# One program for weight folding and the first batch's chain, in an attention kernel on one core

## The reference

```python
xn = _layernorm(x)
kv_c = xn @ W_kvd + b_kvd
q_c = xn @ W_qd + b_qd
q = concatenate([q_c @ W_qu + b_qu, rope(q_c @ W_qr + b_qr)])
k = concatenate([kv_c @ W_ku + b_ku, rope(kv_c @ W_kr + b_kr)])
probs = softmax(where(causal, -1e9, q k^T * scale))
ctx = probs @ (kv_c @ W_vu + b_vu)
out = x + ctx @ W_o + b_o + xn @ bw^T + bias
```

## Time and profile before

| | |
|---|---|
| time, median of 3 runs | 1512.25 us (1511.94 to 1512.78) |
| time of the profiled execution | 1512.11 us |
| its span | 1510.3 us |
| TensorE busy | 1434.2 us, 95% |
| VectorE, ScalarE, GpSimd busy | 1159.1, 1210.5, 947.1 us |
| first instruction of `layer` on TensorE | 97.35 us |
| first instruction of the first step on TensorE | 148.04 us |

### The profile page before, as it was taken

How to read it: one execution, slowest core, us unless ns; L and a number is a source line. 1 busy time by engine, 2 the same in 40 slices (tenths; PEclk the granted TensorE clock), 3 DMA queues, 4 the chain that set the end, 5 groups by cost and what they waited for, 6 DMA issues and landing times.

```text
span 1510.3 us, 27896 instructions
## 1 busy us (share of the span) xinstructions
PE 1434.2 (95%) x9878; PEld 1300.2 (86%) x9878; DVE 1159.1 (77%) x2764; ACT 1210.5 (80%) x2565; POOL 947.1 (63%) x476
## 2 busy tenths in 40 slices
PE   1976999999999999999999999999999999999998
PEld 1855899999889999999889899999889999999987
DVE  2444688888677888888767788888767788888887
ACT  1532788889868888889878888899878888888886
POOL 3010777776767677777767577776866567777750
PEclk9996999999999999999999999999999999999998
DMA  8445232222132432222033432221123422111110
GB/s 209 160 162 124 60 88 60 60 60 60 26 88 71 109 88 60 61 60 60 18 81 84 109 88 60 61 59 46 30 74 95 109 60 60 47 48 49 52 29 29
DMA packets 46819, 111.62 MB, mean 74 GB/s; under 512 B 13600, under 2 KB 22816, under 8 KB 46688
## 3 DMA queue, kind: packets, MB, share of 16 engines
q1 hardware_dynamic: 36912, 103.31, 25.1%
q10 hardware_dynamic: 8720, 3.70, 1.1%
q0 software_dynamic: 1056, 2.89, 0.7%
HBM read 50.10 MB, written 13.63 MB: 42 GB/s over the span
## 4 chain that ended last, share of the span: by engine, by line
PE 81%; ACT 4%; DVE 4%; SPq 1%; POOL 1%; DMA 1%; issue 1%; DVEq 0%; POOLq 0%; ACTq 0%
PE turn L1355 16%; PE ring L1300 11%; PE u_ps L1373 8%; PE ring L1332 8%; PE u_ps L1374 8%; PE ring L1330 8%; PE ring L1331 8%; PE o_ps L1393 4%; PE o_ps L1394 4%; PE ring L1313 2%; PE ring L1262 2%; PE ring L1268 1%; ACT probs L886 1%; DVE probs L1067 1%; DVE probs_lo L1077 1%
## 5 line engine op out<-in xcount | busy, mean ns | idle before, releaser
L1067 DVE TENSOR_SCALAR_CACHE_REDUCE probs<-ring,c_t 128x1024 f32<-128x1024 f32 (+7 forms) x512 | 413.8, 809 | 106.5 <-PE ring L1332 104.1
L1077 DVE TENSOR_TENSOR probs_lo<-turn,probs_hi 128x512 fp32r<-128x512 f32 (+1 forms) x640 | 401.0, 630 | 68.9 <-ACT probs_hi L895 64.2
L895 ACT ACTIVATE probs_hi<-turn 128x512 fp32r<-128x512 f32 (+1 forms) x640 | 351.0, 550 | 113.7 <-PE turn L1355 108.9
L886 ACT ACTIVATE probs<-probs,row_min 128x1024 f32<-128x1024 f32 (+7 forms) x512 | 394.3, 771 | 12.1 <-DVE probs L1067 9.5
L1355 PE MATMUL turn<-ident,probs 128*128 128x128 f32 x2304 | 385.4, 275 | 6.0 <-ACT probs L886 3.7
L1373 PE MATMUL u_ps<-probs_hi,kv_nat 128*128 128x256 f32 x1152 | 314.8, 302 | 0.3 <-DVE probs_lo L1077 0.3
L1355 PEld LDWEIGHTS turn<-ident,probs 128*128 128x128 f32 x2304 | 286.5, 140 | 31.9 <-ACT probs L886 8.9
L1374 PE MATMUL u_ps<-probs_lo,kv_nat 128*128 128x256 f32 x1152 | 290.1, 281 | 0.0
L1330 PE MATMUL ring<-k_hi,q_hi 128*128 128x512 f32 (+2 forms) x768 | 279.8, 364 | 0.0
L1332 PE MATMUL ring<-k_hi,q_lo 128*128 128x512 f32 (+2 forms) x768 | 264.3, 344 | 0.0
L1331 PE MATMUL ring<-k_lo,q_hi 128*128 128x512 f32 (+2 forms) x768 | 262.8, 342 | 0.0
(11 more groups left out here) (174 smaller groups left out, 2623.1 us busy)
## 6 DMA issues: line engine op xcount, KB each, us to landing
wp<-wp_scratch SPq DMA_DIRECT2D x32, 640.0 KB, 4.2
wv<-wv_scratch SPq DMA_DIRECT2D x32, 512.0 KB, 3.4
swapped<-k_rope SPq DMA_DIRECT2D x128, 128.0 KB, 2.3
swapped<-q_y SPq DMA_DIRECT2D x64, 128.0 KB, 2.3
swapped<-q_x SPq DMA_DIRECT2D x64, 128.0 KB, 2.3
wp_scratch<-wp_parts SPq DMA_DIRECT2D x8, 640.0 KB, 3.4
wv_scratch<-wv_parts SPq DMA_DIRECT2D x8, 512.0 KB, 4.2
k_hi<-qb_kv_hi SPq DMA_DIRECT2D x16, 256.0 KB, 3.8
```

The source lines that it names most:

```text
L886: act.activation(p, p, ACT.Exp, scale=-1.0, bias=row_min[:, r:r + 1], accum_out=row_sum[:, g % 4, w, h:h + 1]).then_inc(exp_ready, 1)
L895: act.activation(probs_hi[:, r % 4, 0:width], turn[r % 2][:, 0:width], ACT.Identity).then_inc(turned_hi, 1)
L1067: dve.tensor_scalar(probs_of(g, w, h), ring[slot_of(entry)][:, KEY_COLUMN[qt]:KEY_COLUMN[qt] + keys], c_t[b % 2][:, qt, ds(pair * 2 + h, 1 ...
L1077: dve.tensor_tensor(probs_lo[:, r % 4, 0:width], turn[r % 2][:, 0:width], probs_hi[:, r % 4, 0:width].bitcast(F32), ALU.subtract).then_inc ...
```

## The change

`prepare` and `layer` become one block. The heads are folded one by one, and the chain of the first batch stands between them on every engine.

- TensorE turns heads 0 and 1, then for each i folds head i and turns head i + 2. Behind head 1 come the transposes, behind 2 the down matmuls, behind 5 the projection of the first pair, behind 8 the bias sums, behind 12 and 13 the linear map, and natural at the end. Turned heads lie in the PSUM tensors `turn`, folded ones in `u_ps` and `o_ps`, one head in each.
- ScalarE makes the high parts straight from PSUM (`folded_high`), VectorE the low parts (`folded_low`), both into the parts of the pair. The first pair's parts are `wp` and `wv[0]` themselves; they are stored, but not loaded in the prologue.
- GpSimd scales the rotary weights once and makes their high and low parts (`rope_columns`), and issues the stores (`store_parts`). Before the parts of a pair are written again, the engine that writes waits for the store (`wait_stored`).
- The biases are loaded as rows and turned by one TensorE transpose (`bias_columns` copies them out). x, these rows, the heads, `w_down` and half of W_o are loaded by SP; the other half of W_o by ScalarE; W_qr, W_kr, the binary weights, output biases and rotary tables by GpSimd.
- VectorE sums the values' bias (`value_bias`), head by head; one matmul with ones finishes it (`biases`), as a new entry of the ring.
- The spread of keys to slot 1 moves into the first step, behind a wait for the last two stores; the high and low keys of the second pair also wait for these stores.
- The norm of the first batch is applied half by VectorE, half by ScalarE. Raw weights have two sets of buffers, and share SBUF with the second slots of the main part and its probabilities.

```diff
-            ("project", 0, QUERY_Y), ("linear", 0, 0), ("linear", 0, 1), ("natural", 0, 0), ("natural", 0, 1))
+            ("project", 0, QUERY_Y), ("bias", 0, 0), ("linear", 0, 0), ("linear", 0, 1), ("natural", 0, 0), ("natural", 0, 1))
...
-        prepare(nc, T, x, W_kvd, b_kvd, W_ku, b_ku, W_vu, b_vu, W_kr, b_kr, W_qd, b_qd, W_qu, b_qu, W_qr, b_qr,
-        layer(nc, T, x, wp_dram, wv_dram, out)
...
+        fold_ps = (u_ps[:, :], o_ps[:, :, :].rearrange("p a b -> p (a b)"))
...
+        def parts_of(p):
+
+            return (wp, wv[0]) if p == 0 else (wp_parts[(p - 1) % 2], wv_parts[(p - 1) % 2])
+
+        def wait_stored(engine, p):
+
+            engine.wait_ge(parts_stored[0 if p == 0 else 1 + (p - 1) % 2], 32 * (1 if p == 0 else (p - 1) // 2 + 1))
...
+            def load_heads(turn):
+
+                if turn >= 2:
+                    sp.wait_ge(head_turned, (turn - 1) * LOAD_HEADS)
+                heads = slice(turn * LOAD_HEADS * HD, (turn + 1) * LOAD_HEADS * HD)
+                for to, source in ((qu_a, W_qu[0:P, heads]), (qu_b, W_qu[P:QC, heads]), (ku, W_ku[:, heads]), (vu, W_vu[:, heads])):
+                    sp.dma_start(to[turn % 2][:, :], source).then_inc(turn_loaded[turn % 2], 16)
+
+            def load_row(to, source):
+                sp.dma_start(to, source).then_inc(rows_loaded, 16)
+
+            sp.dma_start(x_sb[:, :, :], x[0].rearrange("(t p) d -> p t d", p=P)).then_inc(x0_loaded, 16)
+            for first, bias in ((B_QU, b_qu), (B_KU, b_ku), (B_VU, b_vu)):
+                load_row(brow[first:first + NH, :], bias.rearrange("(h p) -> h p", p=P))
+            for first, bias in ((B_KR, b_kr), (B_QR, b_qr)):
+                by_head = bias.rearrange("(p h d) -> h p d", h=2, d=RD)
+                load_row(brow[first:first + PAIRS, 0:64], by_head[1])
+                load_row(brow[first:first + PAIRS, 64:P], by_head[0])
+            as_row = lambda bias: bias.rearrange("(a p) -> a p", a=1)
+            load_row(brow[B_DOWN:B_DOWN + 1, :], as_row(b_qd[0:P]))
+            load_row(brow[B_DOWN + 1:B_DOWN + 2, 0:64], as_row(b_qd[P:QC]))
+            load_row(brow[B_DOWN + 1:B_DOWN + 2, 64:P], as_row(b_kvd))
+            load_heads(0)
+            sp.dma_start(w_down[:, :, 0:QC], W_qd.rearrange("(c p) n -> p c n", p=P)).then_inc(down_loaded, 16)
+            sp.dma_start(w_down[:, :, QC:QC + KVC], W_kvd.rearrange("(c p) n -> p c n", p=P)).then_inc(down_loaded, 16)
+            load_heads(1)
+            for c in (2, 3):
+                sp.dma_start(wo[:, c * LOAD_HEADS:(c + 1) * LOAD_HEADS, :],
+                             W_o[c * LOAD_HEADS * P:(c + 1) * LOAD_HEADS * P, :].rearrange("(h p) n -> p h n", p=P)).then_inc(wo_loaded[c], 16)
+            load_heads(2)
+            load_heads(3)
             stack(0)
+            swap(0, 0)
             spread_keys(0)
...
+            def store_parts(p):
+
+                pool.wait_ge(fold_lo, p * 2 + 2)
+                parts, values = parts_of(p)
+                stored_p = parts_stored[0 if p == 0 else 1 + (p - 1) % 2]
+                pool.dma_start(wp_dram[p].bitcast(F32), parts[:, :].bitcast(F32)).then_inc(stored_p, 16)
+                pool.dma_start(wv_dram[p].bitcast(F32), values[:, :, :, :].rearrange("p a b c -> p (a b c)").bitcast(F32)).then_inc(stored_p, 16)
...
+            rope_columns(0)
+            rope_columns(1)
+            rope_columns(2)
+            store_parts(0)
+            store_parts(1)
+            for p in range(3, PAIRS):
+                rope_columns(p)
+                store_parts(p - 1)
+                if p == 5:
+                    residual(0)
+                    pool.wait_ge(residual_ready, NT)
+            store_parts(PAIRS - 1)
             for m in range(STEPS):
                 step(m)
...
+            def head_turned_high(i):
+
+                act.wait_ge(head_turned, i + 1)
+                if i >= 2:
+                    act.wait_ge(fold_full, i - 1)
+                act.activation(turned[i % 2][:, 4 * P:4 * P + 1], cols[:, B_KU + i:B_KU + i + 1], ACT.Identity)
+                act.activation(turned[i % 2][:, 0:4 * P], turn[i % 2][:, :], ACT.Identity).then_inc(turned_w_ready, 1)
+
+            def folded_high(i):
+
+                p, h = divmod(i, 2)
+                act.wait_ge(fold_full, i + 1)
+                if p >= 3 and h == 0:
+                    wait_stored(act, p - 2)
+                f, (parts, values) = fold_ps[i % 2], parts_of(p)
+                folded = f[:, 0:130].rearrange("p (b c) -> p b c", b=2)[:, :, 0:64]
+                act.activation(wq_part(parts, 0)[:, h, :, 64 * h:64 * h + 64], folded, ACT.Identity, scale=-SCALE)
+                act.activation(values[:, h, 0, :], f[:, 256:512], ACT.Identity)
+                act.activation(values[0:64, h, 1, :], f[0:64, 256:512], ACT.Identity).then_inc(fold_hi, 1)
...
+            for i in range(NH):
+                folded_high(i)
+                if i + 2 < NH:
+                    head_turned_high(i + 2)
+                if i == 0:
+                    first_apply()
+                elif i == 1:
+                    leave("transpose", 0, 0)
+                    leave("transpose", 0, 1)
+                elif i == 2:
+                    for k in range(2):
+                        leave("down", 0, k)
+                        down_high(0, k)
+                elif i == 5:
+                    for k in (ROPE_K, QUERY_X, QUERY_Y):
+                        project_left(0, k)
+                elif i == 7:
                     high_keys_of(0)
-                if (what, k) == ("linear", 1):
+                elif i == 10:
...
+            def folded_low(i):
+
+                p, h = divmod(i, 2)
+                to = slice(64 * h, 64 * h + 64)
+                f, (parts, values) = fold_ps[i % 2], parts_of(p)
+                chunks = f[:, 0:130].rearrange("p (b c) -> p b c", b=2)
+                dve.wait_ge(fold_hi, i + 1)
+                dve.scalar_tensor_tensor(out=wq_part(parts, 1)[:, h, :, to], in0=chunks[:, :, 0:64], scalar=-SCALE,
+                                         in1=wq_part(parts, 0)[:, h, :, to].bitcast(F32), op0=ALU.mult, op1=ALU.subtract)
+                dve.tensor_tensor(values[64:P, h, 1, :], f[64:P, 256:512], values[64:P, h, 0, :].bitcast(F32), ALU.subtract)
+                dve.tensor_scalar(bias_p[to, p:p + 1, QUERY_X + h], f[to, 130:131], -SCALE, None, ALU.mult)
+                dve.tensor_scalar(wc_a[:, i:i + 1], chunks[:, 0, 64:65], SCALE, None, ALU.mult)
+                dve.tensor_scalar(nat_wc[0:64, KVC + i:KVC + i + 1], chunks[0:64, 1, 64:65], SCALE, None, ALU.mult).then_inc(fold_lo, 1)
...
+            def value_bias(load):
+
+                dve.wait_ge(wo_loaded[load], 16)
+                for h in range(load * LOAD_HEADS, (load + 1) * LOAD_HEADS):
+                    bias = cols[:, B_VU + h:B_VU + h + 1]
+                    if h == 0:
+                        dve.tensor_scalar(bias_acc[:, :], wo[:, h, :], bias, None, ALU.mult).then_inc(bias_step, 1)
+                    else:
+                        dve.wait_ge(bias_step, h + 1)
+                        dve.scalar_tensor_tensor(out=bias_acc[:, :], in0=wo[:, h, :], scalar=bias, in1=bias_acc[:, :], op0=ALU.mult,
+                                                 op1=ALU.add).then_inc(bias_step, 1)
+
...
+            for i in range(NH):
+                folded_low(i)
+                if i == 2:
+                    first_down_low(0)
+                    first_down_low(1)
+                elif i == 3:
+                    binary_ffn()
+                    value_bias(0)
+                elif i == 4:
+                    value_bias(1)
+                    value_bias(2)
+                elif i == 5:
                     rope(dve, 0, range(0, 3))
-                if (what, k) == ("linear", 0):
-                    rope(dve, 0, range(3, 7))
-                if (what, k) == ("linear", 1):
-                    rope(dve, 0, range(7, ROPE_OPS))
-            low_keys(dve, 0, 1)
-            low_keys(dve, 0, 0)
+                elif i == 6:
+                    value_bias(3)
+                    output_bias()
+                elif i == 7:
+                    low_keys(dve, 0, 1)
+                    low_keys(dve, 0, 0)
+                elif i == 8:
+                    rope(dve, 0, range(3, 8))
+                elif i == 9:
+                    bias_leave()
+                elif i == 11:
+                    rope(dve, 0, range(8, ROPE_OPS))
+                elif i >= 14:
...
+            def turn_head(i):
+
+                load, source = i // LOAD_HEADS, i // LOAD_HEADS % 2
+                columns = slice(i % LOAD_HEADS * HD, (i % LOAD_HEADS + 1) * HD)
+                to = turn[i % 2]
+                if i % LOAD_HEADS == 0:
+                    pe.wait_ge(turn_loaded[source], (load // 2 + 1) * (16 * TURN_DMAS))
+                if i < 2:
+                    pe.wait_ge(cols_ready, 1)
                 else:
-                    begin(what, owner, k)
```

(40 more changed lines are left out.)

626 lines of the change are left out of this document (266 added, 360 removed).

## The result

The kernel after takes 1485.07 us (median of 4 runs, 1483.52 to 1487.06); the kernel before took 1512.51 in runs beside it. The ratio is 0.9818, with a 95% interval of 0.9801 to 0.9835: 27.4 us faster. The forecast was 1472, 40 us faster. The direction and the range held (1457 to 1487, the latter by 2 us); two thirds of the gain came.

What follows compares the result with a forecast made beforehand. TensorE bounds the main steps, which stay; only the stretch before the first step changes. Its terms sum to 116.3 us, less 8 for the clock: 108 against 148.0, so 40 us won, time 1472, range 1457 to 1487.

Steps and rivals of the forecast that it cites:

- TensorE's work: Before the first step: 53.9 us of turns and folds plus 29.6 us of chain work, less 8 for the clock.
- The clock term: Heads after down, projection and linear: dense blocks keep TensorE's clock high for three heads each; net -8 us, bounds 0 to -24.
- rival A: Heads on TensorE: the clock stays high through all 16; S = 95, time 1459, chance 0.2.
- The start: Loads before the first head: first turn at 16 us, plus 1.5 for the first copy, 17.5 in the sum.
- S: Start of the first projection of the second pair, ending the prologue; 148.0 us before, forecast 108.
- VectorE: Between heads: 47 us of work in some 85 stays hidden, except some 1.5 us of TensorE waiting at five rotary operations.
- Stacking: Before the first projection: TensorE waits 8.5 us, between 5 and 12, for four load issues and the stacking DMAs.
- Stores on GpSimd: Stores moved from SP: ScalarE's waits for them are met, except 0.5 us allowed near head 12.
- rival B: Prologue: loads behind x and slow GpSimd stores bind; S = 123, time 1487, chance 0.23.
- Rival D: First step: the 40 us won turn up there as idle time of TensorE; time 1512, chance 0.02.

Runs made afterwards that it cites:

- experiment 3: Kernel after with the first batch's chain behind all 16 heads instead of between them; ratio to before 0.9949.
- experiment 12: Kernel after with the first pair's eight rotary operations on VectorE cut from 1024 columns to 8; ratio to before 0.9808.
- Experiment 2: Kernel after with rows and first heads loaded before x, late-used weights and SP's half of W_o later; ratio to before 0.9787.
- 4: Kernel before with ScalarE's bias columns read as 16 contiguous elements per partition instead of four-byte elements 512 bytes apart; ratio to before 0.9998.
- 1: Kernel after with SP issuing the stacking DMAs before the load of the last four heads; ratio to before 0.9834.
- 7: Kernel after with twelve extra 512-column matmuls on TensorE ahead of its wait for the stacked weights; ratio to before 0.9805.
- 6: Kernel after with stacking DMAs ahead of the last heads' load and VectorE's rotary operations spread over more heads; ratio to before 0.9835.
- 10: Kernel after with VectorE reordered as in experiment 9, and SP's order stack, keys' swap, heads' load, queries' swap, key spread; ratio to before 0.9822.
- 11: Kernel after with the VectorE and SP orders of 10 plus the load order of Experiment 2; ratio to before 0.9787.
- experiment 9: Kernel after with VectorE's bias sums ahead of the keys' rotary and the low keys moved to head 12; ratio to before 0.9813.
- experiment 8: Kernel before with the second slot's keys spread in the first step, behind its first swap, instead of in the prologue; ratio to before 0.9977.

## Why the prediction was right and where it failed

**TensorE's work and its clock: right, and closer than it deserved.** 75.56 measured, 75.5 forecast. By start-to-start times in TensorE's timeline the heads take about 40.5 us (forecast 53.9 - 12.5 = 41.4), the chain 34.8 (forecast 29.6 + 4.5 = 34.1) and the transpose of the rows 0.3 (not in the forecast), so errors of up to 1 us cancel; the largest in a single term is natural, 5.9 instead of 3.9. The clock term, a mere -8 in the forecast's sum, hides the part that experiment 3 shows to be the interleaving's whole worth. The guess that a dense block lifts the clock for some three heads shows in the fold rows of the kernel after (128x256, two at a time; 1.20 us at the lower level, 0.68 at the upper):

```profile
30.80 1.20 PE L1535 MATMUL o_ps<-wo,turned 128*128 128x256 f32 x2
...
36.88 0.68 PE L1535 MATMUL u_ps<-wo,turned 128*128 128x256 f32 x2
...
73.11 0.68 PE L1535 MATMUL u_ps<-wo,turned 128*128 128x256 f32 x2
...
84.14 1.20 PE L1535 MATMUL u_ps<-wo,turned 128*128 128x256 f32 x2
...
103.34 0.68 PE L1535 MATMUL o_ps<-wo,turned 128*128 128x256 f32 x2
```

After transposes and down, after the projection and after linear they are fast. From fold 10 (84.14) they are slow again, through heads 11 and 12 until linear. That is ahead of the pause of 4.20 us, and experiment 12 has slow folds there without it, so the pause is not what costs the clock. Ten of 16 heads are fast: rival A, with all 16, was wrong.

**The start: the step that failed most.** "Not after 9.3 + 9.0 = 18.3 plus an issue" took x and the heads as two transfers, each with the time that it took before. But here all queues shared the 16 DMA engines: they are 95% busy up to 23.5 us at 263 GB/s, and GpSimd's and ScalarE's queues moved some 4 MB of that, for later use. The first heads landed at 23.56. SP's queue shows the delay as slow issues (12.31 and 15.35):

```profile
0.73 0.44 SPq L414 DMA_DIRECT2D x_sb<-in_L_attn_x  x1
...
6.77 0.60 SPq L409 DMA_DIRECT2D vu<-in_L_attn_W_vu  x1
...
12.31 3.00 SPq L409 DMA_DIRECT2D vu<-in_L_attn_W_vu  x1
15.35 5.00 SPq L430 DMA_DIRECT2D wo<-in_L_attn_W_o  x2
```

Experiment 2 moved nothing but the order of these bytes and won 4.7 us of S; 4, in the kernel before, speaks for bytes and against the number of four-byte elements.

**VectorE: hidden on the average, not in its place.** "47 us in a stretch of some 85" was right as a sum (56.20 us are busy up to S, the bias and norm work ahead of the heads among them). But from the landing of the keys' swap the work stands in one piece. VectorE's rows after:

```profile
71.61 1.23 DVE L301 TENSOR_TENSOR k_rope<-k_rope,cos 128x1024 f32<-128x1024 f32 x1 [10.39 <-DMA swapped<-k_rope]
...
79.68 2.47 DVE L311 TENSOR_TENSOR k_lo<-k_rope,k_hi 64x1024 fp32r<-64x1024 f32 x2
...
88.27 1.22 DVE L301 TENSOR_TENSOR q_y<-q_y,swapped 64x1024 f32<-64x1024 f32 x1
89.41 0.28 DVE L1116 SCALAR_TENSOR_TENSOR wp_parts<-o_ps,wp_parts 128x128 fp32r<-128x128 f32 x1
```

Idle for 10.39 us, then without a gap from 71.61 to 92.4. Fold 11 needs the buffer that the last row and the four small ones behind it free, at 90.4. I had 1.5 us there; it was 4.20, and with the other folds 6.7. The idle time before 71.61 cannot be used, since the program's order is fixed; the experiments that advanced TensorE (1, 7) ran into this stretch, and 12 shows its last part by leaving the arithmetic out.

**Stacking: right in kind, 2.1 short.** Four issues of loads take 53.38 to 55.6, as forecast (2.4). From the first stacking issue to the matmul it is then 8.4 us, where the forecast had 6.9 "less 1 since fewer DMAs follow at once": the heads' loads go ahead of them, and the DMA engines are 89% busy in the wait. (Its own terms, 2.4 and 5.9, add up to 8.3, not 8.5.) Undone in 1, it gave back 4.7 us at the projection and 0.6 at S. The wait was on the path and yet worth almost nothing by itself, because the next limiter, the swap and VectorE's rotary, came at nearly the same time as before; the swap, for its part, now met GpSimd's stores.

**Stores on GpSimd: no loss in the kernel after.** Against 3.4 us in the earlier trace rows (and 4.5 for `wv_scratch` in the same view), the page's DMA issues read:

```profile
wp_scratch<-wp_parts POOLq DMA_DIRECT2D x7, 640.0 KB, 3.5
...
wv_scratch<-wv_parts POOLq DMA_DIRECT2D x7, 512.0 KB, 4.4
```

The trap of the Trainium skill that I had weighed (SBUF — State Buffer, "SBUF: two separate sides") is told there for a VectorE operation in a mode that uses both ports, such as an fp32 copy within SBUF. VectorE's long operations beside these stores are tensor_tensors with two inputs, of which the box does not speak, so that no such delay shows here does not test it. A store issued at 80.20, with VectorE busy, took 0.57 us of GpSimd; its partner, issued at 80.77, took 5.8 us to land, the longest of the seven. So the part of rival B that concerned stores failed for this kernel (in 1, 6, 10 and 11 the stores stand beside the late swap), while the part about loads came true. ScalarE does wait 4.07 us for a store at head 10, behind VectorE's rotary, where it costs nothing; experiment 9 made such a wait count.

**Given back.** Rival D exists in small: 1.6 us in the first step. There TensorE's waits for probs, probs_lo and q_y add up to 1.3 us more than before, and GpSimd's rotary starts 0.3 us further behind its swap (4.6 instead of 4.3). The ten kernels with the woven prologue, the one after among them, took 39.0 to 40.6 us from the first swap issue to the second, three with the old one 38.5 to 38.6. The keys for the second slot are not the reason: experiment 8 issues them in the same place and takes 38.5, with the rotary at 4.3. Nor is the weaving: the merged program with its chain in series (3) takes 40.2. What in the merged program makes it stays open.

**What stays open.** Whether GpSimd's stores alone make the keys' swap late. In all four kernels that issue the swap before the stores (1, 6, 10, 11) the stores follow within 0.5 to 0.7 us and the rotary starts 8.2 to 8.3 us behind the swap; in the kernel after, 2, 7, 9 and 12 the stores go first, by 3.7 us or more, and it starts 4.3 to 4.6 us behind. The heads' loads had landed by then in 1 and 6, and the key spread had not been issued in 10 and 11, so neither is common to the four. But no run takes the stores away.

And part of the scatter of 7 us after S. In the kernel after, the tenth, nineteenth and twenty-eighth intervals from one step's keys' swap to the next, counted from the first step's, read 41.4, 41.7 and 41.5 us, where the kernel before has 39.9 each time. At least one of these three is over 41 us in every kernel with the merged program but 7, whose rest of the span is the shortest of them (1360.7), and none is in the three with the old one. The merged program thus loses up to some 5 us there, and no run says why.

## What to carry to other kernels

When independent work is woven into a stretch bound by one engine, sum the busy engine's work first, at the clock that it will have among its new neighbours: here its terms came within some 2 us each, and the whole gain of the interleaving was in them. Look at busy and idle time separately before saying what an edit won. Then go through each other engine's program in its written order, from the DMA that releases it: the wait is set by the longest gapless run between two uses of a double buffer, not by the engine's average load. And add up the bytes that all queues issue in the first microseconds before assuming that one of them lands as it did alone; of the edits to the kernel after that keep its result, those with the new order of loads (2 and 11) were the only ones that took more than 2 us off S.

## What the runs showed of the hardware

GpSimd's small operations stretch beside VectorE's long ones. GpSimd in the kernel after, while VectorE does the queries' rotary:

```profile
87.07 1.26 POOL L534 CAST wp_parts<-kr 128x64 fp32r<-128x64 f32 x1
88.28 1.37 POOL L533 CAST wp_parts<-qr 128x128 fp32r<-128x128 f32 x1
```

The same two casts took 0.24 and 0.29 us in experiment 12, where the rotary was cut short. So a cast seems to be held until a VectorE operation of 1.22 us has ended, which is a reading of these durations and was not tried by itself. It goes the other way too: beside GpSimd's residual, VectorE's two operations of 128x1024 in fp32r at 95.00 and 96.73 took 1.70 and 1.64 us, where the same shape took 1.23 at 47.52. The issue of a store from GpSimd did not stretch (0.53 to 0.57 us with VectorE busy).

A pile of transfers makes a small one late: the four swap DMAs of 128 KB land in 2.3 to 2.4 us in the kernel after (issued from 67.27), and in 2.4 to 6.3 us in experiment 1, where 1152 KB of stores follow 0.5 us behind the first of them and the key spread behind the last.
